# A decoder layer on one core: softmax denominators summed on GpSimd, and ternary feed-forward weights turned during cross-attention

## The reference

```python
x = x + attn(layernorm(x))        # silu(q), silu(k), rotated, masked q k^T v, gate, layernorm
logits = einsum('bhqd,bhkd->bhqk', q, k) * SCALE + bias
attn = softmax(logits, axis=-1)   # over 750 keys
x = x + (attn @ v) @ w_proj
wq = clip(round(w * scale), -1, 1) / scale    # scale = 1 / mean(|w|), for gate, up and down
xq = clip(round(x * s), -128, 127) / s        # s = 127 / max(|x|) of each row
x = x + bitlinear(silu(bitlinear(xn, w_gate)) * bitlinear(xn, w_up), w_down)
```

## Time and profile before

| | us |
|---|---|
| median of 3 runs | 1397.2 (1396.25 to 1398.44) |
| the profiled execution | 1394.94 |
| its span, first to last instruction | 1393.0 |
| TensorE busy | 1236.3 (89%) |
| VectorE busy | 859.3 (62%) |
| ScalarE busy | 562.3 (40%) |
| GpSimd busy | 167.0 (12%) |

### The profile page before, as it was taken

One profiled execution on the slowest core, in us unless ns is written; L12 is line 12 of the kernel. 1 busy time (PEld: TensorE's weight loads), 2 busy tenths in 40 slices (PEclk: granted clock), 3 DMA queues, 4 the chain that ended last, 5 costly groups with the idle time before them and its releaser, 6 DMA issues. The chain is left out here.

```text
span 1393.0 us, 27044 instructions
## 1 busy us (share of the span) xinstructions
PE 1236.3 (89%) x10602; PEld 953.6 (68%) x10602; DVE 859.3 (62%) x1554; ACT 562.3 (40%) x923; POOL 167.0 (12%) x244
## 2 busy tenths in 40 slices
PE   4799989993799999999999999999999973599997
PEld 3687868882677887787887778777878753344443
DVE  5766646654456566566566565565665545788884
ACT  2222222231234334344343334343343334477775
POOL 0011111114001010110111011011101011001110
PEclk9999999996799999999999999999999995999999
DMA  5222242223234243343243341532432218212211
GB/s 157 86 73 86 75 155 89 84 101 112 68 105 104 48 131 82 72 120 96 62 122 81 96 122 45 134 89 66 113 87 68 65 30 291 114 53 68 62 64 40
DMA packets 69142, 129.52 MB, mean 93 GB/s; under 512 B 12720, under 2 KB 25136, under 8 KB 68512
## 3 DMA queue, kind: packets, MB, share of 16 engines
q1 hardware_dynamic: 65880, 117.19, 29.8%
q0 software_dynamic: 3168, 11.01, 2.3%
HBM read 68.96 MB, written 11.22 MB: 58 GB/s over the span
## 5 line engine op out<-in xcount | busy, mean ns | idle before, releaser
L1146 DVE TENSOR_REDUCE xa_m_part<-xa_psM 112x1 f32<-112x376 f32 x512 | 265.5, 546 | 227.7 <-PE xa_psM L1297 223.7
L1073 ACT ACTIVATE space<-xa_psS 125x448 f32<-125x448 f32 x384 | 207.4, 545 | 251.3 <-PE xa_psS L1281 248.0
L1297 PE MATMUL xa_psM<-xa_k,xa_q 104*112 104x376 f32 x512 | 156.2, 350 | 9.5 <-DVE xa_m_part L1146 6.4
L1281 PE MATMUL xa_psS<-xa_q,xa_k 104*125 104x224 f32 x768 | 144.4, 271 | 0.5 <-ACT space L1073 0.5
L1281 PEld LDWEIGHTS xa_psS<-xa_q,xa_k 104*125 104x125 f32 x768 | 136.7, 187 | 7.4 <-issue 1.1
L1321 PE MATMUL xa_psO<-space,cv 125*32 125x224 f32 x1536 | 110.1, 359 | 1.3 <-ACT space L1073 1.3
L1321 PE MATMUL xa_psO<-space,ones 125*32 125x224 f32 x1536 | 107.8, 352 | 0.0
L1297 PEld LDWEIGHTS xa_psM<-xa_k,xa_q 104*112 104x112 f32 x512 | 88.5, 176 | 27.7 <-DVE xa_m_part L1146 11.1
L1267 PE MATMUL xa_psR<-xa_cT_hi,w_hi 128*128 128x376 f32 x256 | 88.2, 344 | 10.0 <-DVE xa_cT_lo L1136 7.7
L1267 PE MATMUL xa_psR<-xa_cT_hi,w_lo 128*128 128x376 f32 x256 | 90.7, 354 | 0.0
L1267 PE MATMUL xa_psR<-xa_cT_lo,w_hi 128*128 128x376 f32 x256 | 87.7, 343 | 0.0
...
## 6 DMA issues: line engine op xcount, KB each, us to landing
xa_k<-xa_k_st SPq DMA_DIRECT2D x384, 94.0 KB, 2.2
...
xa_q<-xa_q_st SPq DMA_DIRECT2D x192, 56.0 KB, 2.0
...
```

The costliest lines, as they stand in the source:

```text
L1073: nc.scalar.activation(pT[:, (s + i) % 2, j], psS[0:KB, (HG * i + j) % NB, 0:2 * N], ACT.Exp).then_inc(exp_done, 1)
L1146: V.tensor_reduce(m_part[:, seg, t, jj:jj + 1], psM[0:T, seg, 0:SEG], AX.X, ALU.max, negate=True).then_inc(mx_read, 1)
L1281: last = M.matmul(psS[0:KB, (HG * i + j) % NB, a * N:(a + 1) * N], k4[0:ROWS, s % 2, j, col:col + KB], q4[0:ROWS, s, j, :], start=True, st ...
L1297: M.matmul(psM[0:T, seg, 0:SEG], q4[0:ROWS, g, jj, t * T:(t + 1) * T], k4[0:ROWS, g % 2, jj, seg * SEG:(seg + 1) * SEG], start=True, stop= ...
```

## The change

Five things are changed together.

1. `attend` loses the products with ones. GpSimd adds the six key tiles of exponentials into p_sum (`sum_keys`, five additions of 125 x 896 a slot), and TensorE multiplies p_sum by ones once, at beat 2 of the next slot (`denominators`). `divide` follows there and writes over o_f; split_heads comes in the next slot. An exponential that overwrites pT now waits for the sums too.
2. A slot has 18 beats. A filler "W" at beat 3 turns one of 24 units (128 x 1024) of the feed-forward weights, in slots 1 to 24. SyncE loads a unit, ScalarE rounds it in two steps at beat 13 (`round_weight`), TensorE turns it as bfloat16 in the next slot, VectorE clips and copies it back, SyncE stores it in DRAM. The weights' scales are made at the start of cross-attention.
3. At the end SyncE loads the turned weights (four transfers, 6 MB) over the query, key and value weights in w_hi and w_lo; ternary_ffn uses them from there and has no weight preparation.
4. The context load moves to GpSimd's queue, `take_shift` from VectorE to ScalarE, the fillers q2 and q3 from slot 0 to the end of slot 3 (q_st has room for two groups only).
5. In the first fillers K0a and K0b come ahead of Xa and Xb, and the first statistics come later on VectorE.

```diff
-def cross_attention(nc, sems, x1, ctx_rows, k_rows, q_rows, x2, shared):
+def cross_attention(nc, sems, x1, ctx_rows, k_rows, q_rows, x2, shared, ffn_weights, w_abs, w_deq):
...
+    SUMS = NK - 1
     LAST_STEP = UNITS - HG
     HALVES = 2 * NT * HG
-    BEATS = 16
+    BEATS = 18
...
+    DENOMINATORS_AT = 2
     TURN_AT = 12
-
-
-    parts_of = {"V": 3, "K": 3, "Y": 3, "q": 1, "r": 1, "X": 1}
+    ROUND_AT = 13
...
+    UNITS_W = 3 * TURNS
+    parts_of = {"V": 3, "K": 3, "Y": 3, "q": 1, "r": 1, "X": 1, "W": 1}
     fill = [
-        {0: "K2a", 3: "K2b", 6: "Xa", 7: "Xb", 8: "Y0", 11: "q2", 12: "q3", 13: "Y1"},
-        {0: "K3a", 3: "K3b", 6: "r0", 7: "r1", 8: "q0", 9: "r2", 10: "r3", 11: "q1", 12: "r4", 13: "r5"},
-        {0: "K0a", 3: "K0b", 6: "V0", 9: "V1", 12: "V2"},
-        {0: "K1a", 3: "K1b", 6: "V3", 9: "V4", 12: "V5"},
+        {0: "K2a", 3: "W", 4: "K2b", 7: "Xa", 8: "Xb", 9: "Y0", 12: "Y1"},
+        {0: "K3a", 3: "W", 4: "K3b", 7: "r0", 8: "r1", 9: "q0", 10: "r2", 11: "r3", 12: "q1", 13: "r4", 14: "r5"},
+        {0: "K0a", 3: "W", 4: "K0b", 7: "V0", 10: "V1", 13: "V2"},
+        {0: "K1a", 3: "W", 4: "K1b", 7: "V3", 10: "V4", 13: "V5", 16: "q2", 17: "q3"},
     ]
-    first_fill = ["r0", "r1", "r2", "r3", "r4", "r5", "Xa", "Xb", "K0a", "K0b", "q0", "q1", "K1a", "K1b", "q2", "q3"]
-    SPLIT_AT = {"q0": 2, "K1a": 3}
+    first_fill = ["r0", "r1", "r2", "r3", "r4", "r5", "K0a", "K0b", "Xa", "Xb", "q0", "q1", "K1a", "K1b", "q2", "q3"]
+    SPLIT_AT = {"K1a": 2, "q3": 3}
...
+            if what == "W":
+                if 1 <= NG * b + s <= UNITS_W:
+                    found[k] = what, NG * b + s - 1
...
-        q_st = sb("q_st", [P, NG, 2, N], F32R)
+        q_st = sb("q_st", [P, 2, 2, N], F32R)
...
-        den = sb("den", [P, N])
+        f_raw = sb("f_raw", [P, WC])
+        f_tern = space[:, 2 * HG * 2 * N:2 * HG * 2 * N + WC // 2].bitcast(BF16)
...
+            def load_ffn(unit):
+                n, t = divmod(unit, TURNS)
+                wait_count(sp, f_tern_ready, unit)
+                w = ffn_weights[n].rearrange("(a p) k -> p a k", p=P)
+                src = w[:, 2 * t:2 * t + 2] if n < 2 else w[:, :, 2 * t * P:2 * (t + 1) * P]
+                sp.dma_start(f_raw[:].rearrange("p (a k) -> p a k", a=src.shape[1]), src).then_inc(f_in, DMA)
+            def store_ffn(unit):
+                n, t = divmod(unit, TURNS)
+                sp.wait_ge(f_out_ready, unit + 1)
...
+                sp.dma_start(dst, f_tern.rearrange("p (k c) -> p k c", k=dst.shape[1])).then_inc(f_stored, DMA)
+            def next_ffn(n):
+                if 1 <= n < UNITS_W:
+                    load_ffn(n)
+                if 1 <= n <= UNITS_W:
+                    store_ffn(n - 1)
+            def load_turned():
+                sp.wait_ge(f_stored, DMA * UNITS_W)
+                for n, w in enumerate((w_hi, w_lo)):
+                    half = slice(n * I // P // 2, (n + 1) * I // P // 2)
+                    sp.dma_start(w[:, 2].rearrange("p k n -> p (k n)").bitcast(BF16),
+                                 down_dram[:, half].rearrange("p a d -> p (a d)")).then_inc(ffn_loaded, DMA)
+                for n, w in enumerate((w_hi, w_lo)):
+                    sp.dma_start(w[:, 0:2].rearrange("p a k n -> p (a k n)").bitcast(BF16),
+                                 gu_dram[n].rearrange("p k i -> p (k i)")).then_inc(ffn_loaded, DMA)

...
             for b in range(B):
-                if b >= 1 and b + 1 < B:
-                    load_context(b + 1)
+                next_ffn(NG * b)
                 pack_keys(b, 2)
+                next_ffn(NG * b + 1)
                 if b + 2 < B:
                     load_x(b + 2)
                 pack_keys(b, 3)
                 load_residual(b)
+                next_ffn(NG * b + 2)
                 if b + 1 < B:
                     pack_queries(b + 1, 0)
                     pack_keys(b + 1, 0)
+                    next_ffn(NG * b + 3)
                     pack_keys(b + 1, 1)
                     pack_queries(b + 1, 1)
+            load_turned()
+            sp.wait_ge(ffn_loaded, 4 * DMA)
...
+            def sum_keys(b, s):
+                n = NG * b + s
+                wait_count(pool, den_full, n)
+                for m in range(SUMS):
+                    i, a = divmod(m + 1, 2)
+                    tile = pT[:, (s + i) % 2, :, a * N:(a + 1) * N]
+                    if m in (0, 1, 3):
+                        wait_apart(pool, exp_done, UNITS * n + HG * (i + 1), pool_passed)
+                    before = pT[:, s % 2, :, 0:N] if m == 0 else p_sum[:]
+                    if m > 0:
+                        pool.wait_ge(p_summed, SUMS * n + m)
+                    nc.gpsimd.tensor_tensor(p_sum[:], before, tile, ALU.add).then_inc(p_summed, 1)
+                pool.wait_ge(p_summed, SUMS * (n + 1))
+            def load_context(b):
+                wait_count(pool, pv_done, NB * NG * (b - 1))
+                pool.dma_start(cv[:, b % 2], ctx_rows[b].rearrange("(a p) d -> p a d", p=KB)).then_inc(c_in, DMA)
...
             for b in range(B):
                 for s in range(NG):
+                    if (b, s) != (0, 0):
+                        split_heads(*((b, s - 1) if s > 0 else (b - 1, NG - 1)))
+                    if s == 0 and b >= 1 and b + 1 < B:
+                        load_context(b + 1)
+                    if s == 1 and b >= 1:
+                        store(b - 1)
+                    if s == 3 and b + 2 < B:
+                        rstd(b + 2)
+                    sum_keys(b, s)
                     if b + 1 < B:
                         clear_shift(b, s)
-                    split_heads(b, s)
-                    if s == 0 and b >= 1:
-                        store(b - 1)
-                    if s == 2 and b + 2 < B:
-                        rstd(b + 2)
+            split_heads(B - 1, NG - 1)
...
+                    if g >= 2:
+                        act.wait_ge(q_packed[0], QPACK * (b + 1))
+                    elif b >= 1:
+                        act.wait_ge(q_packed[1], QPACK * b)
+                    copy(q_st[:, g % 2, 0], src[:, 0:N], SCALE).then_inc(high[r], 1)
...
+            def take_shift(n):
+                act.wait_ge(maxima_turned, n + 1)
...
+            def round_weight(unit):
+                n = unit // TURNS
+                if unit == 0:
+                    act.wait_ge(const_made, 4)
+                    act.wait_ge(w_scale_step, 3)
+                act.wait_ge(f_in, DMA * (unit + 1))
+                nc.scalar.activation(f_raw[:], f_raw[:], ACT.Identity, bias=magic[:, 0:1], scale=w_inv[:, n:n + 1]).then_inc(f_rounded, 1)
+                act.wait_ge(f_rounded, unit + 1)
+                wait_count(act, f_stored, DMA * unit)
+                nc.scalar.activation(f_tern, f_raw[:], ACT.Identity, bias=magic[:, 1:2]).then_inc(f_tern_ready, 1)

             def exponentials(b, s, i, j):
                 n = NG * b + s
                 if j == 0 and NB * n + i >= 2:
                     act.wait_ge(pv_done, NB * n + i - 1)
+                    act.wait_ge(p_summed, SUMS * n + (-2, 0, 1)[i])
...
+                        if k == TURN_AT and NG * b + s + 1 < NG * B:
+                            take_shift(NG * b + s + 1)
+                        if k == ROUND_AT and NG * b + s < UNITS_W:
+                            round_weight(NG * b + s)
...
+                if what[0] == "W":
+                    dve.wait_ge(full[r], use_of[what, b])
+                    V.tensor_scalar(f_tern, src.bitcast(BF16), -1.0, 1.0, ALU.max, ALU.min).then_inc(f_out_ready, 1)
+                    dve.wait_ge(f_out_ready, b + 1)
+                    dve.sem_inc(read[r], 1)
...
             def divide(b, s):

                 n = NG * b + s
-                dve.wait_ge(pv_done, NB * (n + 1))
-                V.reciprocal(den[:], psO[:, DEN:DEN + N]).then_inc(den_ready, 1)
+                dve.wait_ge(den_full, n + 1)
+                wait_count(dve, oT_ready, n)
+                V.reciprocal(o_f[:], psO[:, DEN:DEN + N]).then_inc(den_ready, 1)
                 dve.wait_ge(den_ready, n + 1)
-                wait_count(dve, oT_ready, n)
-                V.tensor_tensor(o_f[:], psO[:, 0:N], den[:], ALU.mult).then_inc(o_ready, 1)
+                V.tensor_tensor(o_f[:], psO[:, 0:N], o_f[:], ALU.mult).then_inc(o_ready, 1)
...
-                if what == "r1":
+                if what == "r4":
                     statistics(0)
+                if what == "K0a":
                     normalise(0)
                 if what in SPLIT_AT:
                     split_weight(SPLIT_AT[what])
                 take(what, 0)
             statistics(1)
             normalise(1)
+            dve.wait_ge(w_totalled, 1)
+            V.tensor_scalar(w_mean[:], psO[:, 0:3], 1.0 / (I * D), TINY, ALU.mult, ALU.max).then_inc(w_scale_step, 1)
+            dve.wait_ge(w_scale_step, 1)
+            V.reciprocal(w_inv[:], w_mean[:]).then_inc(w_scale_step, 1)
```

(63 more changed lines are left out.)

164 lines of the change are left out of this document (58 added, 106 removed).

## The result

The changed kernel takes 1424.92 us (median of 4, 1420.52 to 1426.19) against 1397.82 for the kernel before on the same chip: a ratio of 1.0185, 95% interval 1.0162 to 1.0209. The forecast was 1358. Its profiled execution has a span of 1418.9 us, 25.9 more than before; the forecast had it 39.2 less.

What follows compares the result with a forecast made beforehand. TensorE's order of work was taken to bound cross-attention, and a chain of weight preparation the stretch before the feed-forward loop. The terms summed to -39.2 us: 1355.7 from the profiled execution, 1358 on the median's footing, range 1330 to 1386.

Steps and rivals of the forecast that it cites:

- SyncE's and GpSimd's queues: Cross-attention transfers: stores wait for turned copies, the context load hides in GpSimd's idle time; no cost, slack 1 us.
- fourth rival: SyncE's queue in slot s=2 late by 3 us a batch: +21 us, 1379; chance 0.12.
- Feed-forward start, -34.5: Stretch before the feed-forward loop: weight preparation leaves it, -34.5 us, if the weights lie in SBUF by then.
- fifth rival: Feed-forward start: the weights come back late and up to 20 us return, 1378; chance 0.05.
- The sums, 2.10 us each: GpSimd in cross-attention: each addition of 125 x 896 takes 2.10 us, bounds 1.9 and 3.1, work hidden.
- sixth rival: Cross-attention: the sums are dear and GpSimd becomes the bound, +75 us, 1433; chance 0.07.
- TensorE's work, -73 + 16 + 17: Cross-attention: products with ones removed -73 us, denominators added +16, turned weight units added +17; net -40.
- Hand-over, 0.55 a slot, +16: Division at beat 2 delays VectorE's reductions; TensorE waits 0.55 us in each of 29 full slots, +16.
- second rival: Cross-attention: the waits at the division and behind ScalarE's roundings cost nothing, 1334; chance 0.20.
- ScalarE's queue, 2.5 before K0a: Slot s=1: context tiles stand behind roundings; TensorE waits 2.5 us in place of 1.1, +8.4 over six batches.
- third rival: Cross-attention slots: VectorE's join of maxima is caught behind GpSimd's second or third sum, +25 us, 1383; chance 0.10.
- The tail, +6.3: Last two slots, without TensorE fillers: GpSimd's cycle of 15.1 us shows, 39.5 us in place of 33.2, +6.3.

Runs made afterwards that it cites:

- e1: The changed kernel with GpSimd's context load split into two transfers, of 112 and 13 partitions; 1371.6 us.
- e6: The changed kernel without weight units in cross-attention, feed-forward stage as before, context load split into 112 and 13 partitions; 1389.52 us.
- e10: The changed kernel with the context load split into 112 and 13 partitions and the reductions moved away from the division; 1362.1 us.
- e8: The changed kernel with context load split (112 and 13 partitions), reductions moved from the division, rounding in slot s=1 at beat 16, not 13; 1352.09 us.
- e3: The changed kernel with the weight units beside the context load cut, the loaded to 16 of 1024 columns, the stored to 16 of 128 partitions; 1400.55 us.

## Why the prediction was wrong, step by step

**The step that failed** is "SyncE's and GpSimd's queues": "No cost, slack 1 us", and of the context load "seven more of them hide in its idle time". It priced the issue of the transfers and not their run, and so put the wait for keys at nothing. GpSimd did have the time (1.63 us to issue one), and SyncE did issue the last key in time. But the load was then 5 us nearer to the keys' need, with a weight unit between it and the keys, and in the kernel before these keys had landed 0.26 us ahead of their need (batch 3). TensorE waited 45.0 us for them, and the clock fell each time. It cost 53 us: 1424.9 less 1371.6. No row of the context load's transfer was among those I read; the earlier trace rows has only the keys'. The fourth rival, SyncE's queue late, had the right neighbourhood and 3 us a batch instead of 10, in another slot and for another reason; e1 shows that SyncE's order was not it. One of the prediction's own signs of being wrong did come: batches above 99 us (105.7 to 108.8).

**With that load split, the rest stands at 1371.6, 13.6 over the forecast, though within the range.** By the profiled spans, e1's is 22.5 below that of before where I had 39.2:

- **Feed-forward start, -34.5: right.** Before, from rows rounded to the scale of the hidden rows, it took 51.0 us. Now (changed kernel, VectorE):

```profile
1227.37 0.43 DVE L1735 TENSOR_SCALAR ff_xq<-ff_xm 128x512 bf16<-128x512 f32 x1
1242.45 0.15 DVE L1727 TENSOR_SCALAR ff_h_scale<-ff_h_inv 128x1 f32<-128x1 f32 x1
```

14.8 us, so -36.2. The last weights landed at 1188.3 (issued 1170.86, 17.5 us), 39 us before the first rounded rows: the fifth rival did not come.

- **The sums, 2.10 us each: right.** The page:

```profile
L1094 POOL TENSOR_TENSOR xa_p_sum<-xa_p_sum,space 125x896 f32<-125x896 f32 x128 | 270.7, 2115 | 109.8 <-ACT space L1189 104.4
```

TensorE waits for p_sum only in the last slots, three times. The sixth rival is out. (The lower bound of 1.9 in the prediction is 2.0 by its own rule, 4.556 x 896 / 2048.)

- **TensorE's work, -73 + 16 + 17: net too large by a third.** One batch by windows (batch length, busy time of each engine), first before:

```profile
sum 96.20, PE 93.60 PEld 76.82 DVE 58.83 ACT 38.10 POOL 10.86; mean PE 93.60 PEld 76.82 DVE 58.83 ACT 38.10 POOL 10.86
```

then e6, the sums without weight units:

```profile
sum 94.00, PE 87.88 PEld 71.25 DVE 53.73 ACT 41.27 POOL 54.65; mean PE 87.88 PEld 71.25 DVE 53.73 ACT 41.27 POOL 54.65
```

and e1, with both:

```profile
sum 95.90, PE 90.41 PEld 73.37 DVE 56.20 ACT 50.27 POOL 54.72; mean PE 90.41 PEld 73.37 DVE 56.20 ACT 50.27 POOL 54.72
```

The sums took 5.7 us of work out of a batch where the terms give 7.1. The four weight units of a full batch put 2.5 in where the terms give 2.8. Over eight batches and 24 units that is -31 in place of -40, 9 us. An attend block fell from 1.66 to 0.89 us, as summed. The group of denominators is dearer: e1's starts at 715.42, the next product at 715.94, and both start about 0.1 late by their neighbours' pace, so some 0.7 in place of 0.50, which is 0.8 of the 1.4 us that a batch lacks; where the rest sits I did not resolve.
- **Hand-over, 0.55 a slot, +16: right in size, and the second rival out.** The waits for m_part are 27.2 us in 39 (24.9 in e1), against 6.4 in 17 before; in a slot the one at the division is 0.62. It is not a fixed price, though: e10 moves two products and has 8.9.
- **ScalarE's queue, 2.5 before K0a: right,** 2.34. The row copy (4 x 896) takes 0.91, taken as 1.0. The term of 8.4 was still too large for the waits: before, a batch had two for cT_lo, 1.10 and 0.65, and the second is gone, so the rise is 0.6 a batch, 3.5 in six. That e8's later rounding was worth 10 us, with the clock in it, comes near 8.4 by luck.
- **join_maxima caught behind a sum (third rival): not in full slots.** L1277 has a median of 0.168 as before. Three of its 32 are longer, 0.75 in the first batch (423.0), 0.73 and 1.19 in the tail (1164.0 and 1181.1, each while a sum ran on GpSimd); before, none is above 0.17.
- **The tail, +6.3: too small.** From the last logits of slot (7,1), 1163.5, to the last split, 1206.7, it took 43.2 us, not 39.5. The last two slots took 17.6 and 15.7 by the divisions, not 15.1 each. In e1 they took 18.8 and 15.7. From the join for slot (7,0) to the first rounded rows e1 needs 113.1 us against 97.7 before: this stretch and the seven batches ahead of it (-6.5 measured) are 14.6 over what I had for them together (-5.7). The term above is 9 of it, and the tail, 44.4 us in e1 in place of 39.5, is 5.
- **The start, +1:** the first join is at 405.9 in the changed kernel and at 403.6 in e1, against 399.9: +6.0 and +3.7.

Left open: how much of the delay on the five engines is due to the number of pieces that share them and how much to bytes. One weight unit more is 32 KB for each, 1.3 us at 25 GB/s, and the store 16 KB, 0.7 us, while batch 6, which lacks the one and has fewer pieces of the other, is 10 us shorter; the packets under e3 go a good part of the way. And the load itself: 1500 KB and five sixteenths of the 768 KB of weights and 1128 KB of keys make 17 us at 125 GB/s, not 22.5 (its packets run from 724.07 to 743.51 in batch 3).
